# Head of a fused attention and FP4 feed-forward kernel: order of the stacks, the late x and v

## The reference

```python
x_proj = silu(x @ W1 + b1)
u, v, q, k = split(x_proj, 4)
attn = silu(einsum('bqhd,bkhd->bhqk', q, k)) / S        # no softmax
av = einsum('bhqk,bkhd->bqhd', attn, v)
x = layernorm(x + (layernorm(av * u) * gamma + beta) @ W2 + b2)
gate, y = fp4_linear(x, w_gate), fp4_linear(x, w_up)    # FP4 quantised in blocks of 16
x = layernorm(x + fp4_linear(silu(gate) * y, w_down))
```

## Time and profile before

| | us |
|---|---|
| three runs, median | 515.42 |
| lowest, highest | 514.72, 517.13 |
| the profiled execution | 514.83 |
| its span (first to last instruction) | 513.0 |
| what lies around the span | 1.8 |

### The profile page before, as it was taken

How to read it: one execution, slowest core, us unless ns; L and a number is a source line. 1 busy time by engine, 2 the same in 40 slices (tenths; PEclk the granted TensorE clock), 3 DMA queues, 4 the chain that set the end, 5 groups by cost and what they waited for, 6 DMA issues and landing times.

```text
span 513.0 us, 20141 instructions
## 1 busy us (share of the span) xinstructions
PE 495.9 (97%) x9030; PEld 263.9 (51%) x9032; DVE 281.4 (55%) x738; ACT 487.4 (95%) x548; POOL 56.9 (11%) x148
## 2 busy tenths in 40 slices
PE   9899999999999999999999999999999999999996
PEld 5443344444353444434354444434477777777762
DVE  6546642755748475665847475574343443544445
ACT  5999999999999999999999999999999999999940
POOL 7620000001010100101010100101010101101010
PEclk9999999999999999999999999999999999999999
DMA  7932340000000000000000000000000000000000
GB/s 190 231 85 60 96 134 3 1 3 7 3 6 3 8 2 3 6 1 8 3 7 3 8 1 3 6 4 6 3 8 4 9 4 10 9 3 9 4 3 12
DMA packets 15156, 12.39 MB, mean 24 GB/s; under 512 B 1783, under 2 KB 14718, under 8 KB 15070
## 3 DMA queue, kind: packets, MB, share of 16 engines
q1 hardware_dynamic: 14088, 9.44, 7.5%
q0 software_dynamic: 688, 1.40, 1.1%
q10 hardware_dynamic: 294, 0.26, 0.2%
HBM read 1.92 MB, written 1.05 MB: 6 GB/s over the span
## 4 chain that ended last, share of the span: by engine, by line
ACT 51%; PE 31%; issue 15%; DVE 2%; POOL 0%; POOLq 0%; DVEq 0%
ACT attn L643 50%; PE ps L405 29%; PE ps L419 2%; PE ps L448 1%; ACT v_sb L643 0%; POOL rstd_b L388 0%; DVE xn_b L769 0%; DVE stats_b L799 0%; ACT feat L643 0%; DVE xn_b L777 0%; DVE xn_b L773 0%; DVE xn_b L775 0%; POOLq L141 0%; DVE magic_b L771 0%; POOL ve_b L387 0%
## 5 line engine op out<-in xcount | busy, mean ns | idle before, releaser
L643 ACT ACTIVATE attn<-ps 128x1024 f32<-128x1024 f32 x512 | 475.8, 1211 | 0.3 <-PE ps L405 0.2
L405 PE MATMUL ps<-attn,v_pad 128*32 128x256 f32 (+1 forms) x5120 | 274.4, 341 | 0.3 <-DVE wdown_t L979 0.2
L405 PE MATMUL ps<-q_stack,k_stack 64*128 64x256 bf16 (+1 forms) x2560 | 173.6, 251 | 10.4 <-ACT attn L643 1.5
L405 PEld LDWEIGHTS ps<-attn,v_pad 128*32 128x32 f32 x5120 | 132.2, 109 | 80.2 <-issue 39.6
L405 PEld LDWEIGHTS ps<-q_stack,k_stack 64*128 64x128 bf16 x2560 | 78.6, 94 | 133.5 <-ACT attn L643 87.1
L387 POOL TENSOR_TENSOR ve_a<-mv_a,eps_col 128x1 f32<-128x1 f32 x24 | 4.6, 191 | 230.2 <-DVE mv_a L801 230.2
L387 POOL TENSOR_TENSOR ve_b<-mv_b,eps_col 128x1 f32<-128x1 f32 x24 | 4.6, 191 | 202.7 <-DVE mv_b L801 202.7
L742 DVE CAST parts<-feat 128x512 bf16<-128x512 f32 (+1 forms) x10 | 3.8, 383 | 25.3 <-ACT feat L643 25.3
L405 PE MATMUL ps<-zeros 128*128 128x512 bf16 x46 | 12.2, 412 | 1.4 <-DVE zeros L916 1.2
L388 POOL TENSOR_TENSOR rstd_a<-ve_a,minus_half 128x1 f32<-128x1 f32 x24 | 13.3, 555 | 1.9
L388 POOL TENSOR_TENSOR rstd_b<-ve_b,minus_half 128x1 f32<-128x1 f32 x24 | 13.3, 555 | 1.9
(11 more groups left out here) (183 smaller groups left out, 405.6 us busy)
## 6 DMA issues: line engine op xcount, KB each, us to landing
q_stack<-parts SPq DMA_DIRECT2D x18, 128.0 KB, 2.4
k_stack<-parts SPq DMA_DIRECT2D x15, 128.0 KB, 3.8
x_sb<-in_L_attn_x SPq DMA_DIRECT2D x3, 256.0 KB, 5.1
k_stack<-zeros SPq DMA_DIRECT2D x6, 128.0 KB, 5.4
q_stack<-zeros SPq DMA_DIRECT2D x6, 128.0 KB, 2.4
k_stack<-parts SPq DMA_DIRECT2D x9, 64.0 KB, 2.7
q_stack<-parts SPq DMA_DIRECT2D x9, 64.0 KB, 2.0
out<-x_a SPq DMA_DIRECT2D x8, 64.0 KB, 1.5
```

Of the source, the lines that this page charges most:

```text
L405: return pe.matmul(to, lhsT, rhs, start=start, stop=stop, skip_group_check=True)
L643: return act.activation(to, frm, ACT.Silu, **kw)
```

## The change

- `HEAD` loses the transposes of x from 1280 and 1792 and the second v, and makes k 256 ahead of the transpose of x from 768. The second v becomes a job at step 0, the two transposes jobs at steps 2 and 3, and nearly all later jobs of the first column move by one or two steps. VectorE copies the two late transposes to `xT` instead of ScalarE.
- SP issues the stacks k 0, q 0 and k 256 ahead of the two late loads of x, and then the stack of k 768 ahead of the zero rows of k 1280 and k 1792. No DMA writes zeros for k 256 and k 768: GpSimd clears those parts of `k_stack` by memsets. The one for k 256 stands where it cleared the first quarter of `v_pad`; those for k 768 stand between its share of the stacks and its first pad. VectorE clears the first quarter of `v_pad` in two halves.
- Of the stack of q 0, ScalarE issues the three DMAs of the first part, behind its copy of x from 256, SP two, and GpSimd one.
- GpSimd pads the second v ahead of the loads of weights.
- TensorE makes products of zeros in the head: one behind the transposes of x from 0, two behind those of x from 256, two behind k 768.

```diff
-    PREP_AT = {2: ("k", 1280), 5: ("v", 2), 7: ("k", 1792), 9: ("v", 3), 11: ("u", 0), 13: ("q", 256),
-               15: ("u", 1), 17: ("q", 512), 19: ("u", 2), 21: ("q", 1024), 23: ("u", 3), 25: ("q", 1536),
-               27: ("w2", 0), 29: ("gate", 0), 31: ("up", 0), 33: ("down", 0)}
+    PREP_AT = {0: ("v", 1), 2: ("xT", 1280), 3: ("xT", 1792), 4: ("k", 1280), 6: ("v", 2), 8: ("k", 1792), 10: ("v", 3),
+               12: ("u", 0), 14: ("q", 256), 16: ("u", 1), 18: ("q", 512), 20: ("u", 2), 22: ("q", 1024),
+               24: ("u", 3), 26: ("q", 1536), 28: ("w2", 0), 30: ("gate", 0), 32: ("up", 0), 33: ("down", 0)}
...
-        HEAD = [("xT", 0, 256, 0), ("k", 0, 256, 1), ("q", 0, 256, 2), ("xT", 256, 512, 3), ("xT", 768, 512, 4),
-                ("k", 256, 512, 5), ("xT", 1280, 512, 7), ("xT", 1792, 256, 0), ("v", 0, 512, 6),
-                ("k", 768, 512, 7), ("v", 512, 512, 6)]
+        HEAD = [("xT", 0, 256, 0), ("k", 0, 256, 1), ("q", 0, 256, 2), ("xT", 256, 512, 3), ("k", 256, 512, 5),
+                ("xT", 768, 512, 4), ("v", 0, 512, 6), ("k", 768, 512, 7)]
+
+        FILL = {("xT", 0): (1, 7), ("xT", 256): (2, 7), ("k", 768): (2, 4)}
...
-        SHARES = [((0, 1, 4), (2, 5, 3)), ((0, 2, 5), (1, 4, 3)), ((0, 1, 4), (2, 5, 3))]
+        SHARES = [((0, 1, 4), (2, 5, 3)), ((2, 5), (3,)), ((0, 1, 4), (2, 5, 3))]
+        BY_ACT = (0, 1, 4)
...
@@ SP's queue
-            sp.wait_ge(zeros_ready, 1)
-            for n in range(3, len(X_LOADS)):
-                load_x(sp, n)
-            zero_rows(sp, unit_no[("k", 256)])
-            sp.wait_ge(stack_zeroed, 2)
-            for n in range(3):
-                stack(sp, n, SHARES[n][0])
-            for start in (768, 1280, 1792):
+            sp.wait_ge(stack_zeroed, 2)
+            for n in range(2):
+                stack(sp, n, SHARES[n][0])
+            sp.wait_ge(k_zeroed, 1)
+            stack(sp, 2, SHARES[2][0])
+            load_x(sp, 3)
+            load_x(sp, 4)
+            sp.wait_ge(k_zeroed, 3)
+            stack(sp, unit_no[("k", 768)])
+            sp.wait_ge(zeros_ready, 1)
+            for start in (1280, 1792):
                 zero_rows(sp, unit_no[("k", start)])
+            for start in (1280, 1792):
                 stack(sp, unit_no[("k", start)])
...
@@ GpSimd
+            def zero_k(start, w):
+                pool.memset(k_stack[:, :, start:start + w].bitcast(U32), 0).then_inc(k_zeroed, 1)
...
-            pool.memset(v_pad[:, 0:TPC, :, :], 0.0).then_inc(v_zeroed_early, 1)
+            zero_k(256, 512)
...
             for n in range(3):
                 stack(pool, n, SHARES[n][1], by_pool=True)
+            zero_k(768, 256)
+            zero_k(1024, 256)
...
             pad_v(0)
+            pad_v(1)
...
-            pad_v(1)
             pad_v(2)
...
@@ TensorE, the head and the jobs
+            def turn_x(bank, start, w):
+                pe.wait_ge(x_loaded[X_LOADS.index((start, w))], 16)
+                for i in range(w // P):
+                    last = pe.transpose(ps[:, bank, i * P:(i + 1) * P], x_sb[:, start // P + i, :], ident[:, :])
+                return last
+
+            def multiply_zeros(times, bank):
+                for _ in range(times):
+                    mm(ps[:, bank, :], zeros[:, 0:P], zeros[:, :])
...
+                multiply_zeros(*FILL.get((kind, start), (0, 0)))
             pe.wait_ge(head_act, xT_all)
...
+                elif kind == "xT":
+                    last = turn_x(bank, i, X_LOADS[[a for a, _ in X_LOADS].index(i)][1])
...
@@ ScalarE, the head
+                if (kind, start) == ("xT", 256):
+                    act.wait_ge(split_done, 3 * unit_no[("q", 0)] + 1)
+                    for t in BY_ACT:
+                        act.dma_start(q_stack[t::8, :, 0:256], parts[:, unit_no[("q", 0)] % PARTS, 0, 0:256]).then_inc(stacked_by_act, 16)
...
@@ VectorE
             dve.tensor_copy(b1_col[:, 1:3], ps[:, 6, 1:3]).then_inc(b1_ready, 1)
+            zero_first_v(0)
+
+            def copy_xT(start):
+                bank = wait_made("xT", start, None)
+                w = X_LOADS[[a for a, _ in X_LOADS].index(start)][1]
+                dve.tensor_copy(xT[:, start:start + w], ps[:, bank, 0:w]).then_inc(job_by_vec, 1)
...
             split("k", 256)
+            zero_first_v(1)
             split("k", 768)
+            copy_xT(1280)
+            copy_xT(1792)
             zero_v(1)
+            zero_v(2)
             split("k", 1280)
-            zero_v(2)
+            zero_v(3)
...
             split("k", 1792)
-            zero_v(3)
```

More of the change, by code:

```diff
@@ L221, in build @@
         split_done = sem("split_done")
-        stack_zeroed, v_zeroed_early, v_zeroed, v_padded = (sem("stack_zeroed"), sem("v_zeroed_early"), sem("v_zeroed"),
-                                                            sem("v_padded"))
+        stack_zeroed, k_zeroed, v_zeroed_early = sem("stack_zeroed"), sem("k_zeroed"), sem("v_zeroed_early")
+        v_zeroed, v_padded = sem("v_zeroed"), sem("v_padded")
         stacked = [sem(f"stacked{n}") for n in range(len(UNITS))]
+        stacked_by_act = sem("stacked_by_act")
         stacked_by_pool = [sem(f"stacked_by_pool{n}") for n in range(3)]
@@ L246, in build @@
         head_no = {job[:2]: n for n, job in enumerate(HEAD)}
-        X_LOADS = [(job[1], job[2]) for job in HEAD if job[0] == "xT"]
+        X_LOADS = [(0, 256), (256, 512), (768, 512), (1280, 512), (1792, 256)]
         xT_all = max(n for n, job in enumerate(HEAD) if job[0] == "xT") + 1
@@ L270, in stack @@
                     eng.dma_start(to[t::8, :, start:start + w], parts[:, n % PARTS, part, 0:w]).then_inc(done, 16)
-        SHARES = [((0, 1, 4), (2, 5, 3)), ((0, 2, 5), (1, 4, 3)), ((0, 1, 4), (2, 5, 3))]
-        BY_DMA = [len(SHARES[0][0]), len(SHARES[1][0]), len(SHARES[2][0]) + HD - TERMS]
+        SHARES = [((0, 1, 4), (2, 5, 3)), ((2, 5), (3,)), ((0, 1, 4), (2, 5, 3))]
+        BY_ACT = (0, 1, 4)
         def wait_stack(eng, n):
+            if n == 1:
+                eng.wait_ge(stacked_by_act, 16 * len(BY_ACT))
             if n < len(SHARES):
-                eng.wait_ge(stacked[n], 16 * BY_DMA[n])
+                eng.wait_ge(stacked[n], 16 * len(SHARES[n][0]))
                 eng.wait_ge(stacked_by_pool[n], 16 * len(SHARES[n][1]))
             else:
-                eng.wait_ge(stacked[n], 16 * HD)
+                eng.wait_ge(stacked[n], 16 * (TERMS if n == unit_no[("k", 768)] else HD))
         def w1_by_feature(i):
@@ L352, in pad_v @@
                 else:
-                    pool.wait_ge(v_zeroed_early, 1)
+                    pool.wait_ge(v_zeroed_early, 2)
                 if ("v", c * CH) in head_no:
@@ L434, in project_v @@
                                start=False)
+            def turn_x(bank, start, w):
[6 more added lines that the diff above has]
+                    mm(ps[:, bank, :], zeros[:, 0:P], zeros[:, :])
             pe.wait_ge(zeros_ready, 1)
-            for _ in range(WARM_UP):
-                mm(ps[:, 7, :], zeros[:, 0:P], zeros[:, :])
+            multiply_zeros(WARM_UP, 7)
             pe.wait_ge(ident_ready, 1)
@@ L445, in _ @@
                 if kind == "xT":
-                    pe.wait_ge(x_loaded[X_LOADS.index((start, w))], 16)
-                    for i in range(w // P):
-                        last = pe.transpose(ps[:, bank, i * P:(i + 1) * P], x_sb[:, start // P + i, :], ident[:, :])
+                    last = turn_x(bank, start, w)
                 else:
@@ L606, in keep_warm @@
             def keep_warm(piece):
-                for _ in range(KEEP_WARM.get(piece, 0)):
-                    mm(ps[:, 2, :], zeros[:, 0:P], zeros[:, :])
+                multiply_zeros(KEEP_WARM.get(piece, 0), 2)
             r = TAIL_ROWS
@@ L912, in to_out, with zero_first_v @@
                 finish(tile)
+            def zero_first_v(half):
+                tiles = slice(half * TPC // 2, (half + 1) * TPC // 2)
+                dve.memset(v_pad[:, tiles, :, :], 0.0).then_inc(v_zeroed_early, 1)
             dve.memset(zeros[:, :], 0.0).then_inc(zeros_ready, 1)
```

2 lines of the change are left out of this document (added).

## The result

The changed kernel took 518.75 us (median of 17 executions, 517.43 to 520.74), the kernel before 516.19 on the same chips (17 executions, 514.62 to 518.21): a ratio of 1.0058 with a 95% interval of 1.0042 to 1.0073. It is slower, by about 3.0 us (0.0058 x 516.19), where 515.0 and a range of 513.8 to 516.7 were forecast.

A forecast was written before the change was run, and what follows sets the result against it. ScalarE and TensorE, both busy nearly the whole span, were taken as the bound. Start -0.90, second v +0.49, old idle -0.16 gave -0.57, taken as -0.4: 514.4 us profiled, median 515.0, range 513.8 to 516.7.

The forecast's parts named there:

- First activation: Start of the loop: ScalarE's first activation of scores at 13.9 instead of 14.80, a gain of 0.9 us.
- k feature at 10.45: Head: ScalarE starts the k feature at 10.45, 0.43 later than before, behind three DMA issues of 0.63 each.
- rival D: Head: fills raise TensorE's clock early, k 0 and q 0 each 0.43 shorter; -1.2 us, median 514.2; chance 0.10.
- its own sign of being wrong (14.4): Start of the loop: the prediction would be wrong if the first activation of scores is not before 14.4.
- the copy of x from 768: Head: ScalarE's copy, needed by TensorE, ends at 11.74, just in time.
- Step 2 needs the second k stack: Step 2: k 256 stack lands at 17.0, bounds 16.4 and 17.7; covered, costing 0.1 at 17.7.
- The k 1280 stack: Step 10: split from 24.8 to 27.4, issued by SP to 29.3, lands near 32.5, when wanted.
- All else: Loop: weights behind the second pad, later zero rows and the v_pad clear have 2 us of slack or more; cost 0.
- the far end, double: GpSimd's clears of two parts of k_stack take 3.5 us instead of 1.76, costing 1.3.
- B: Early steps: TensorE's order binds, having gained 2.04 us of jobs; about no change, 514.8 to 515.2 profiled; chance 0.22.
- C: Steps 2 and 3: TensorE's transpose waits for late x, landing at 20.6; 1.6 us slower, median 517.0; chance 0.12.
- three points without slack: Scores of steps 5 and 10 and the k stack from 1280 arrive just when due; -0.57 was therefore taken as -0.4.

The follow-up runs named there:

- weights late: Changed kernel, but GpSimd issues the nine weight loads behind the third pad of v instead of the second; 518.00 us, ratio 1.0036.
- split first: Changed kernel, but VectorE splits k 1280 ahead of clearing the third quarter of v_pad; 519.86 us, ratio 1.0072.
- all three edits: Changed kernel with k 1280 split before the clear, late x issued ahead of all stacks, weights behind the third pad; 517.31 us, ratio 1.0016.
- plain v: Changed kernel, but the v job of step 0 is made in whole width instead of strips; 518.14 us, ratio 1.0025.
- four edits: Changed kernel with v job of step 0 in whole width, late x ahead of stacks, weights behind third pad, k 1280 split before the clear; 515.60 us, ratio 0.9987.
- plain v and x early: Changed kernel with the v job of step 0 in whole width and late x issued ahead of all stacks; 516.67 us, ratio 1.0010.
- x early: Changed kernel, but SP issues the two late loads of x ahead of all stacks; 518.82 us, ratio 1.0051.
- the profile with the zeros: Changed kernel with eight products of zeros on TensorE before the wait for the k 256 stack at step 2; 518.15 us, ratio 1.0030.
- the kernel before with strips: Kernel before the change, with the head's second v made in strips of 32 columns, 54 more TensorE instructions ahead of step 2; 516.66 us, ratio 0.9999.

## Why the prediction was wrong

**The start came out by luck.** First activation 13.9 forecast, 13.73 measured; k feature at 10.45 forecast, 10.54 measured. ScalarE's three issues took 2.28 us, 0.76 each, and not the 0.63 of SP's row, but inside the bound of 0.8. They began 0.36 earlier than I had it, since the granted clock rose early in this execution: k 0 and q 0 ran as rival D had them, in 1.12 us where the kernel before took 2.07:

```profile
5.05 1.12 PE L424 MATMUL ps<-xT,w_qk 128*128 128x256 f32 x4
```

It gained nothing more, because ScalarE's k feature waited behind those issues. But 13.9 was the forecast for a clock that rises late, as in the kernel before. In the profile of the kernel with the weights late, which has the same head, it did:

```profile
5.45 1.91 PE L425 MATMUL ps<-xT,w_qk 128*128 128x256 f32 x4
14.39 2.86 ACT L672 ACTIVATE attn<-ps 128x1024 f32<-128x1024 f32 x3
```

The loop starts at 14.39 there, and at 14.45 to 14.49 in the three other profiles of changed kernels in which these products took 1.91 (split first, all three edits, plain v). So under its own condition the walk missed by 0.5, past its bound of 13.9, and at its own sign of being wrong (14.4). The issues began at 8.86 and not 8.57, behind the new zeros, and took 2.3 and not 1.88; the copy of x from 768, "just in time" at 11.74, ended near 12.4, and TensorE waited 0.39 for it. A gain of 0.3 to 0.4 is less than the second v's activation, which cost 0.48 (0.49 forecast).

**The step that failed first** is "Step 2 needs the second k stack ... I take 3.5 us, 13.5 + 3.5 = 17.0, bounds 16.4 and 17.7". It landed at 18.6. I had reasoned that late x is "no longer ahead in the queues", and didn't ask what it does right behind. The last DMA took 3.5 us with nothing beside it (three profiles: all three edits, four edits, plain v and x early), 4.2 with x behind it (plain v), 5.2 with the fetch (x early), and with both 5.0 here, 5.2 and 5.3 in two others (split first, weights late), but 4.2 in the profile with the zeros. The value was right for a case that this kernel isn't. The fetch I could not have priced, but it is in the trace of before.

**The term that was missing altogether** is the clock behind a wait. I weighed it in rival D alone, for the head, as a gain, and left out that TensorE could lose it in the loop, where the change lengthened the wait of step 2. Behind the wait of 2.96 us the next product was 0.86 longer (1.93 less 1.07), and behind the wait of 1.90 the one at 38.32 took 1.63 and the v job's 1.95 where 1.07 and 1.06 are usual. Zeros in the first wait gave back 1.4 us, though with the stack 0.8 us sooner in that profile; in the kernel before they gave a ratio of 0.9974 with the stack where it was.

**The k 1280 stack** was forecast for 32.5 and landed at 37.7. "All else (weights issued behind the second pad ...) has 2 us of slack or more: 0" failed: with the weights beside it the last DMA took 5.05 us where 2.4 was measured without them. It failed by the walk's own times: with the second pad ending at 24.0 to 24.7 and nine issues behind it (5.3 us before, from 15.19 to 20.46), the weights fall beside a stack issued up to 29.3. The rest of its lateness was handed on from steps 2 and 3: the split began at 28.75 and not at 24.8. I had seen that it had no slack and put 0.17 on it; what has no slack passes on every earlier delay in full.

**GpSimd.** Its two clears took 1.84 us where 1.76 was taken, and the far end, double, is excluded. The first pad took 2.29, longer than the 1.68 used, and ended at 18.26, still before the stack. The second I had put at 1.0 to 1.7. GpSimd's timeline, and VectorE's beside it:

```profile
15.97 2.29 POOL L381 COPY v_pad<-v_sb 128x128 f32<-128x128 f32 x4
26.75 1.00 POOL L381 COPY v_pad<-v_sb 128x128 f32<-128x128 f32 x4 [8.50 <-DVE v_pad L972]
```

```profile
14.59 1.60 DVE L774 CAST parts<-feat 128x512 bf16<-128x512 f32 x1
...
27.07 1.76 DVE L972 MEMSET v_pad<- 128x2048 f32 x1 [0.38 <-issue]
```

It took 1.00 with VectorE's clear running through most of it, and 2.29 beside the splits; a cast of VectorE that takes 0.43 elsewhere took 1.60 beside GpSimd's clears. By the rule of the Trainium skill ("SBUF — State Buffer", section Who interferes with whom), that a clear of VectorE leaves the shared ports alone, and that its casts (in a two-port mode) and its instructions with two SBUF inputs do not, the trace agrees: the row of 1.68 that I used for a pad beside a clear was of the wrong neighbour. TensorE waited for neither pad here, but the second, held until 26.75 by VectorE's late clear, sent the weights out from 27.70 on, beside the k 1280 stack.

**The rivals.** B, that TensorE's jobs take its lead, may be the background of all this: with more lead the waits could have been absorbed, which no run here tests by itself. But it was priced at "no change", and jobs alone don't show as a cost: with the transfers mended and the same jobs, one of them in whole width, the kernel is level with before (0.9987). C, the late x, was right about the load: it took 6.1 us where my walk had 4.1. But the transpose came later still, and x did its harm to the stack ahead of it; its 1.6 us came near the size for the wrong reason. Its second half is seen with the zeros, a wait of 0.91. My sum of idle time was "under 0.2", 6.05 was measured. The chance of 0.05 for slower by over 0.5% was too low, as the walk had three points without slack, and I priced each as if the others held.

**What stays open.** What makes the fetch come some records sooner or later with the same program; why the stack took 4.2 us and not 5.0 in the profile with the zeros; and how the 3.0 us of the median divide among x, fetch, weights and clock: they are not additive (x early alone 0.4 us, on top of the plain v 0.8, neither clear of the noise). The clock can't be all of it: the three executions of the changed kernel with a mean clock of 1.000 took 517.4 to 517.7, and the eight shortest of the kernel before 514.6 to 515.9.

## What to carry to other kernels

A transfer issued behind an urgent one can still slow it, and so can one from another engine's queue (4.2 us against 3.5 with x behind, 5.05 against 2.4 with GpSimd's weights beside): ask what is in flight from the urgent issue to its landing, the program's own instruction fetches included, not only what is ahead. A stall of TensorE is paid twice where its clock falls behind it. A few products of zeros in a wait that can't be removed cost little here, and four of them (ratio 0.9974) did more than the whole change as it was made (1.0058). And where a walk through the timeline ends in several arrivals "just in time", the forecast is not their common case but the first of them to slip.

## What was not expected of the hardware

One packet of TensorE's instructions (16 KB, queue 8) went with one late share of the 16 of a 128 KB DMA, which landed behind the other 15 by 0.6 us in the changed kernel, 1.6 with x early and 0.2 with the zeros. The wait for the DMA ends with the last share (18.59 and 18.64 in the changed kernel). Adding 54 instructions ahead of step 2 moved the packet from 19.5 to 17.1 us in the kernel before, and taking them out moved it from 16.3 to 20.7 in the changed one; some of either is the clock, which rose earlier in one profile of each pair.

ScalarE's DMA issues took 0.76 us each against 0.60 to 0.63 on SP's and GpSimd's queues for the same kind of transfer.

The granted clock fell around waits of TensorE of 1.46 and 0.49 us (four edits), and of 1.27, 0.68 and 1.16 us within 4.4 us (the kernel before with strips); in the profile with all three edits a wait of 1.44 us had no fall behind it, though eight of its twelve executions have a mean clock of 0.994 or 0.995. With four to eight products of zeros in the wait no execution out of 48, of four kernels, had a mean clock under 0.997, and four of them were at 0.997. When the clock first rises in the head also differs from one profile to the next, with the same instructions of TensorE up to there (1.03 to 1.91 us for the four products of k 0 and q 0 in the changed kernels).
